# Degree power ahead of the border masks, constants and first tiles loaded as the first instructions, no clearing blocks

## The chip, the cores and the metric

One core of a Trainium2 chip. The metric is the device time of one execution in microseconds, the median of three runs. TensorE (PE) does the matmuls, VectorE (DVE), ScalarE (ACT) and GpSimd (POOL) the elementwise work, and SyncE (SP) issues the transfers. Each engine works through its own queue of instructions in order and waits on semaphores.

## What is computed

Four graph layers over x of 64 x 128 x 128 (batches, nodes, features) with one adjacency of 128 x 128. Each is followed by a residual sum and a layer norm. The first needs all eigenvectors U of a normalized Laplacian:

```python
deg = jnp.sum(A, axis=0) + jnp.sum(A, axis=1) - jnp.diagonal(A)
d_inv_sqrt = jnp.where(deg > 0, jax.lax.rsqrt(deg), 0.0)
L_norm = d_inv_sqrt[:, None] * (jnp.diag(deg) - A) * d_inv_sqrt[None, :]
_, U = jnp.linalg.eigh(L_norm)
h = jax.nn.relu(jnp.einsum('mn,bnd->bmd', U.T, x) @ W1 + b1)
x = _layernorm(x + jnp.einsum('nm,bmd->bnd', U, h @ W2 + b2))
x = _layernorm(x + gcn_then_lstm_over_windows(x, adj))   # windows of 1, 2, 3 and 4 nodes
x = _layernorm(x + graph_attention(x, adj))
x = _layernorm(x + four_head_masked_attention(x, adj))
```

## The kernel before

The program is a sequence of blocks. A block gives each engine a stream of instructions and ends in a barrier of all engines; the next block begins behind it.

**Block one**, `spectral_basis` (L52), makes the Laplacian and brings it to tridiagonal form in 127 reflections that are written out one after the other, with VectorE, TensorE, ScalarE and GpSimd working on each in turn. SyncE's part is one transfer, `A` (L129). GpSimd first fills tiles (L134 to L141), makes the identity and the triangle `below` (L143, L145), then six masks `blocks` (L151) and seven `borders` (L156, L159), and then raises the degrees to the power -0.5 (L162); after that come its two instructions of each reflection, `open_tail` (L167) and `open_gain` (L170). VectorE's path is: diagonal, row sums and degrees (L238 to L245), a wait for the power, and L248 to L258, which make the Laplacian M and the first reflection's column. `borders` is read in block two only.

**A clearing block** (`clear_semaphores`, L1434) follows block one, and another follows block two. GpSimd clears each semaphore that the block before it used, with one instruction each (L1438); the other engines go to the barrier at once.

**Block two**, `spectral_vectors` (L334). GpSimd makes tables (L408 to L424), on which VectorE waits (`tables`), and then seven `joins` (L427). TensorE and ScalarE build the basis in seven levels (L440 to L448), turn the constants of the layers (`turn`, after waiting for all 16 loads) and, once VectorE has finished its first count, multiply the features by W1 in 16 groups (`multiply`); the products go to DRAM and are read back later as `xw`. VectorE meanwhile finds the eigenvalues by counting sign changes (four counts) and makes the eigenvectors; the last instructions copy U and UT (L631, L632). SyncE's part: the 16 loads of the constants (`load`, L715), two `x_here` (L795), and then, for each group, the product's store and the load of the group after next (`transfer`, L798, L801).

**The layers** (`layers`, L836) run four trips over four slots of four batches each. The first trip's first stage is a matmul of `xw` with U in each slot (`hidden`; the helper's line is L1049). SyncE starts by loading `xin` (from x) and `xw` (the products) for the four slots (L1003, L1004); TensorE waits for both tiles of a slot and for a semaphore, `banks_free`, that VectorE raises as its first act:

```python
pe.wait_ge(x_in[s], trip * 32 + 32)
on("banks_free", s, trip)
each(P[s][1], lambda b: xw[s][:, b, :], lambda b: U[:]).then_inc(S_("hidden_ready"), 1)
```

Of the kernel before, what the change touches and what calls it, by code (L numbers as in the profile page):

```python
# [11 lines left out]
ALU = mybir.AluOpType  # L12
# [3 lines left out]
N = 128  # L16
# [34 lines left out]

def spectral_basis(nc, sb, psum, sem, adj_dram, A, ident_tail, ones, reflectors, gains, borders):  # L52

# [6 lines left out]
    E = sb("E", [N, N])  # L60
# [36 lines left out]
    stored = sem("stored")  # L97
    v_ready = sem("v_ready")
    row_copied = sem("row_copied")
# [14 lines left out]
    def col(j, n=1):  # L114
        return small[:, j:j + n]
# [10 lines left out]
    with nc.Block() as block:  # L126
        @block.sync
        def _(sp):
            sp.dma_start(A[:], adj_dram).then_inc(adj_in, 16)  # L129

        @block.gpsimd
        def _(pool):
            t = Tally(pool, pool_step)
            t.done(nc.gpsimd.memset(ident, 0.0))  # L134
            t.done(nc.gpsimd.memset(below[:], 1.0))
            t.done(nc.gpsimd.memset(ones[:], 1.0))
            t.done(nc.gpsimd.memset(tiny[:], 1e-30))
# [195 lines left out]

def spectral_vectors(nc, sb, psum, sem, ident, ones, E, D, reflectors, gains, borders, U, UT, constants, products):  # L334

# [51 lines left out]
    norm_ready = sem("ynorm_ready")  # L387
    y_ready = sem("y_ready")
    yT_ready = sem("yT_ready")
# [6 lines left out]

    load, turn, keep, mark = constants
# [239 lines left out]
G = 4  # L637
# [39 lines left out]

def load_constants(nc, c, sb_here, psum, sem, d, A, ident, ones):

# [6 lines left out]
    WT = sb_here("WT", [H, H])  # L686
    blockP = [psum(f"blockP{j}", [N, 512]) for j in range(4)]
    loads = sem("constants_in")
# [21 lines left out]
              (raw_b[:, 0, :], d["L1_gnn_bih"].rearrange("p (g r) -> (p g) r", r=H)),  # L710
              (raw_b[:, 1, :], d["L1_gnn_bhh"].rearrange("p (g r) -> (p g) r", r=H))]

    def load(sp):
# [58 lines left out]

    return load, turn, keep, mark


def feature_products(nc, sb, psum, sem, c, ident, x_dram, products_dram):

# [5 lines left out]
    made = [sb(f"made_{j}", [N, G, H]) for j in range(2)]  # L783
    acrossP = psum("acrossP", [N, 512])
    madeP = psum("madeP", [N, 512])
    fetched = [sem(f"fetched_{j}") for j in range(2)]
# [17 lines left out]

    def multiply(pe):
        for k in range(groups):
            j = k % 2
# [12 lines left out]

    def keep(act):
        for k in range(groups):
            j = k % 2
# [8 lines left out]

    return transfer, multiply, keep


def layers(nc, sb, psum, sem, c, ident, U, UT, x_dram, products_dram, out_dram):  # L836

    p4 = products_dram.rearrange("(t s g) n d -> t s n g d", s=SLOTS, g=G)
    x4 = x_dram.rearrange("(t s g) n d -> t s n g d", s=SLOTS, g=G)
    out4 = out_dram.rearrange("(t s g) n d -> t s n g d", s=SLOTS, g=G)  # L840
    GH = G * H
# [3 lines left out]

    xin = tiles("xin", [N, G, H])
    xw = tiles("xw", [N, G, H])
    x = tiles("x", [N, G, H])
# [35 lines left out]
    constant_ready = sem("constant_ready")  # L884
    x_in = [sem(f"x_in_{s}") for s in range(SLOTS)]
    y_out = [sem(f"y_out_{s}") for s in range(SLOTS)]
# [528 lines left out]
def program(nc, d, out):  # L1415
    from contextlib import ExitStack
    with ExitStack() as whole:
# [6 lines left out]
        def sem_of(stack):  # L1424
            def get(name):
                used.append(stack.enter_context(nc.semaphore(name)))
                return used[-1]
            return get

        used = []  # L1430
# [10 lines left out]
        sb = sb_of(whole)  # L1441
        A = sb("A", [N, N])
# [5 lines left out]
        c = hold_constants(sb)  # L1448
        products_dram = nc.dram_tensor("feature_products", (B, N, H), F32, kind="Internal").ap()
        with ExitStack() as spectrum:  # L1450
# [3 lines left out]
            borders = [held(f"borders_{1 << level}", [N, N]) for level in range(LEVELS)]  # L1454
            with ExitStack() as part:
                E, D = spectral_basis(nc, held, psum_of(part), sem_of(part), d["adj"], A, ident_tail, ones, reflectors, gains,
                                      borders)
                clear_semaphores()
            with ExitStack() as part:
                constants = load_constants(nc, c, sb_of(part), psum_of(part), sem_of(part), d, A, ident, ones)  # L1460
                products = feature_products(nc, sb_of(part), psum_of(part), sem_of(part), c, ident, d["x"], products_dram)
                spectral_vectors(nc, sb_of(part), psum_of(part), sem_of(part), ident, ones, E, D, reflectors, gains, borders,
                                 U, UT, constants, products)
                clear_semaphores()
        with ExitStack() as part:
            layers(nc, sb_of(part), psum_of(part), sem_of(part), c, ident, U, UT, d["x"], products_dram, out)

# [16 lines left out]
```

## Time and profile before

| | |
|---|---|
| three timed runs | 1472.52, 1474.07 and 1478.42 us, median 1474.07 |
| the profiled execution | span 1472.2 us, from its first to its last instruction; no other time of it is given |
| busy: PE, DVE, ACT, POOL | 1049.8, 1125.0, 803.6, 173.0 us |
| granted TensorE clock, mean | 0.895 |
| DMA packets | 25.51 MB, mean 17 GB/s |

The engines' busy times are sums over stages in which different engines lead, and they overlap. The chain of waits, which the profile follows back from the last instruction, reaches back to 670.2 us, the opening of the layers; what comes before it is read from the timeline and the waits.

### The profile page before, as it was taken

To read this page: it belongs to the slowest core of one execution; us is meant where nothing else is said; L and a number is where in the kernel's file an instruction comes from. 1 tells how busy PE (TensorE), PEld (TensorE's weight loads), DVE (VectorE), ACT (ScalarE), POOL (GpSimd) and SP (SyncE) were. 2 spreads that over 40 slices of the span, in tenths; PEclk is the share of its full clock that TensorE was granted. 3 is DMA by queue.
4 is the path that set the end of the run, shared out by engine and by line. 5 is a ranking of instruction groups with operands and counts; after the bars stand their busy time and mean duration, and the time that the engine had idled before them with its cause. 6 is when DMAs were issued, how large, how long until landed. Compare 5 with 4: busy or idle time off the path is not lost.

```text
span 1472.2 us, 24898 instructions
## 1 busy us (share of the span) xinstructions
PE 1049.8 (71%) x6161; PEld 862.0 (59%) x6161; DVE 1125.0 (76%) x5634; ACT 803.6 (55%) x2921; POOL 173.0 (12%) x464
## 2 busy tenths in 40 slices
PE   5777777777655600006998779988789978899875
PEld 4666666666544500005797566976668966679754
DVE  6888888888799889994457785576865578845687
ACT  3555555555322200003677866767767778677786
POOL 2111111111200000001011110111020120201111
PEclk9999999999986555557999999999899989999998
DMA  0000000000123400004000011000030000100001
GB/s 2 1 1 1 1 1 1 1 1 1 37 54 101 115 1 1 0 1 115 1 1 1 2 32 57 1 2 1 1 88 1 2 1 1 30 1 1 1 1 29
DMA packets 45246, 25.51 MB, mean 17 GB/s; under 512 B 1921, under 2 KB 44066, under 8 KB 45090
## 3 DMA queue, kind: packets, MB, share of 16 engines
q1 hardware_dynamic: 45090, 23.81, 5.8%
q8 instruction: 51, 0.84, 0.2%
q14 instruction: 105, 0.86, 0.2%
HBM read 15.42 MB, written 8.39 MB: 16 GB/s over the span
## 4 chain that ended last, share of the span: by engine, by line
PE 31%; DVE 11%; ACT 8%; issue 3%; POOL 1%; DMA 0%; DVEq 0%; POOLq 0%; ACTq 0%; SPq 0%
PE P L1101 11%; PE P L1109 6%; PE P L1049 6%; PE P L1054 2%; ACT x L1203 2%; ACT S L1271 2%; DVE stats L1310 2%; DVE S L1382 1%; DVE top L1387 1%; PE P L1163 1%; DVE t L1400 1%; PE P L1118 1%; PE P L1147 1%; POOL t L1037 1%; ACT t L1251 1%
## 5 line engine op out<-in xcount | busy, mean ns | idle before, releaser
L193 PE MATMUL productP<-M,ident_tail 128*128 128x127 f32 (+63 forms) x254 | 87.3, 441 | 71.2 <-DVE M L313 71.2
L1101 PE MATMUL P<-t,WihT 128*128 128x128 f32 (+1 forms) x832 | 119.4, 290 | 10.9 <-POOL t L1037 10.9
L1109 PE MATMUL P<-step_h,WhhT 128*128 128x128 f32 (+2 forms) x768 | 123.4, 304 | 0.0
L193 PEld LDWEIGHTS productP<-M,ident_tail 128*128 128x128 f32 x254 | 63.6, 311 | 95.0 <-DVE M L313 95.0
L1101 PEld LDWEIGHTS P<-t,WihT 128*128 128x128 f32 x832 | 109.9, 191 | 14.5 <-POOL t L1037 13.7
L1223 ACT ACTIVATE gate_i<-P,half_bias 128x128 f32<-128x128 f32 (+3 forms) x160 | 69.2, 433 | 88.9 <-PE P L1109 65.0
L1030 POOL TENSOR_TENSOR rstd<-variance,minus_half 128x4 f32<-128x4 f32 x64 | 64.5, 1008 | 430.8 <-DVE variance L1320 430.8
L1109 PEld LDWEIGHTS P<-step_h,WhhT 128*128 128x128 f32 x768 | 108.9, 191 | 4.5 <-DVE step_h L1353 0.7
L464 PE MATMUL sumP<-ident_tail,Yb 128*128 128x128 f32 x1 | 0.5, 473 | 153.2 <-DVE Yb L627 153.2
L190 PE MATMUL tailP<-ident_tail 128*128 128x128 f32 (+63 forms) x254 | 87.7, 443 | 19.9 <-DVE ident_tail L297 8.8
L1340 DVE SCALAR_TENSOR_TENSOR gate_i<-gate_i,gate_g 128x128 f32<-128x128 f32 (+2 forms) x96 | 36.1, 376 | 83.7 <-ACT gate_g L1223 83.7
L1271 ACT ACTIVATE S<-S,ntop 128x128 f32<-128x128 f32 x256 | 98.6, 390 | 0.0
L464 PEld LDWEIGHTS sumP<-ident_tail,Yb 128*128 128x128 f32 x1 | 0.2, 183 | 153.5 <-DVE Yb L627 153.5
L190 PEld LDWEIGHTS tailP<-ident_tail 128*128 128x128 f32 x254 | 63.6, 311 | 44.0 <-DVE ident_tail L297 42.9
L198 PE MATMUL p_rowP<-M,v_col 128*128 128x127 f32 (+63 forms) x254 | 84.9, 432 | 0.9 <-DVE v_col L282 0.7
L1101 PE MATMUL P<-HT,WihT 128*128 128x256 f32 (+1 forms) x288 | 84.7, 433 | 0.0
L220 ACT ACTIVATE small<-M,small 128x1 f32<-128x1 f32 x127 | 37.4, 294 | 84.2 <-DVE small L278 84.2
L494 ACT ACTIVATE small<-small 128x1 f32<-128x1 f32 x1 | 0.2, 203 | 149.1 <-DVE small L600 149.1
L1203 ACT ACTIVATE x<-x,shift,rstd 128x128 f32<-128x128 f32 x192 | 78.7, 483 | 4.3 <-POOL shift L1032 3.9
L215 ACT ACTIVATE row_square<-tailP 128x128 f32<-128x128 f32 (+63 forms) x127 | 28.8, 227 | 90.7 <-PE tailP L190 90.7
L1223 ACT ACTIVATE gate_o<-P,half_bias 128x128 f32<-128x128 f32 (+3 forms) x160 | 70.4, 440 | 8.5 <-PE P L1118 8.5
L1337 DVE SCALAR_TENSOR_TENSOR cell<-gate_i,gate_g 128x512 f32<-128x512 f32 (+3 forms) x64 | 27.9, 436 | 57.0 <-ACT gate_g L1223 56.4
(326 smaller groups left out, 3222.5 us busy)
## 6 DMA issues: line engine op xcount, KB each, us to landing
x_here<-x SPq DMA_DIRECT2D x16, 256.0 KB, 3.1
feature_products<-made SPq DMA_DIRECT2D x16, 256.0 KB, 2.4
xin<-x SPq DMA_DIRECT2D x16, 256.0 KB, 2.9
xw<-feature_products SPq DMA_DIRECT2D x16, 256.0 KB, 3.2
out<-y SPq DMA_DIRECT2D x16, 256.0 KB, 2.3
W<-L_gnn_W SPq DMA_DIRECT2D x3, 64.0 KB
Wqkv<-L_gnn_W SPq DMA_DIRECT2D x1, 192.0 KB
Wg<-L_gnn_Wg SPq DMA_DIRECT2D x2, 64.0 KB
```

Source lines behind the costliest of these rows:

```text
L190: pe.matmul(tailP[:, now:N + 1], tails, ident_tail[:, now:N + 1], start=True, stop=True).then_inc(tail_row_ready, 1)
L193: pe.matmul(productP[:, remaining], tails, M[:, remaining], start=True, stop=True).then_inc(product_ready, 1)
L198: pe.matmul(p_rowP[:, remaining], reflector, M[:, remaining], start=True, stop=True).then_inc(p_row_ready, 1)
L220: nc.scalar.activation(col(BETA_M), M[:, now:now + 1], ACT.Copy, scale=col(BETA)).then_inc(beta_m_ready, 1)
L1030: nc.gpsimd.tensor_tensor(rstd[s][:], variance[s][:], minus_half[:], ALU.pow).then_inc(S_("rstd_ready"), 1)
L1049: last = pe.matmul(out[:, b * H:(b + 1) * H], lhs(b), rhs(b), start=True, stop=True)
L1101: last = pe.matmul(place, c["WihT"][:, p - 1, gate * H:(gate + 1) * H], sources(s, p, t), start=bank not in fresh, stop=not t, skip_group_ ...
L1109: last = pe.matmul(gate_place(s, p, t, gate), c["WhhT"][:, p - 1, gate * H:(gate + 1) * H], step_h[s][:, 0:G * windows(p)], start=False, s ...
L1203: last = A_.activation(to[s][:, b, :], x[s][:, b, :], ACT.Identity, bias=shift[s][:, b:b + 1], scale=rstd[s][:, b:b + 1])
L1223: return A_.activation(tile[s][:, 0:m], gate_place(s, p, t, gate), ACT.Tanh, bias=bias[:, k:k + 1], scale=scale)
L1271: last = A_.activation(S[s][:, h, b, :], S[s][:, h, b, :], ACT.Exp, bias=ntop[s][:, k:k + 1], accum_out=total[s][:, k:k + 1])
L1340: V.scalar_tensor_tensor(gi[s][:, 0:m], gi[s][:, 0:m], 1.0, gg[s][:, 0:m], ALU.add, ALU.mult)
```

## The change

Three things. GpSimd computes the degree power right after the triangle masks, ahead of `blocks` and `borders`. SyncE issues the 16 constants, the first two `x_here` and the four first `xin` in block one, behind A, and the four first `xw` at the end of its part of block two; the layers' own first loads are gone. The clearing blocks are gone: all semaphores are taken for the whole program, and two that shared a name with one of the layers are renamed. The tiles that are loaded early are taken early too; the PSUM banks of the constants and the products are still taken in block two.

```diff
         def _(sp):
             sp.dma_start(A[:], adj_dram).then_inc(adj_in, 16)
+            for begin in fetch:
+                begin(sp)
...
             nc.gpsimd.memset(col(EXPONENT), -0.5).then_inc(masks_ready, 1)
+            pool.wait_ge(deg_base, 1)
+            nc.gpsimd.tensor_tensor(col(DI), col(DEG), col(EXPONENT), ALU.pow).then_inc(deg_root, 1)
             for level in range(1, LEVELS):
...
                 nc.gpsimd.tensor_tensor(borders[level][:], wider, blocks[level - 1][:], ALU.subtract)
-
-            pool.wait_ge(deg_base, 1)
-            nc.gpsimd.tensor_tensor(col(DI), col(DEG), col(EXPONENT), ALU.pow).then_inc(deg_root, 1)
...
         def _(sp):
-            load(sp)
             transfer(sp)
+            first_inputs(sp)
...
-    def transfer(sp):
+    def fetch(sp):
         for k in range(2):
             sp.dma_start(x_here[k][:], x_groups[k]).then_inc(fetched[k], 16)
+
+    def transfer(sp):
         for k in range(groups):
...
             on = waiter(sp)[0]
-            for s in range(SLOTS):
-                sp.dma_start(xin[s][:], x4[0, s]).then_inc(x_in[s], 16)
-                sp.dma_start(xw[s][:], p4[0, s]).then_inc(x_in[s], 16)
             with sp.Fori(0, TRIPS - 1) as i:
...
-        def clear_semaphores():
-
-            with nc.Block() as block:
-                @block.gpsimd
-                def _(pool):
-                    for semaphore in used:
-                        pool.sem_clear(semaphore)
-            used.clear()
...
+        def first_residuals(sp):
+            for s in range(SLOTS):
+                sp.dma_start(xin[s][:], by_slots(d["x"])[0, s]).then_inc(x_in[s], 16)
+
+        def first_products(sp):
+            for s in range(SLOTS):
+                sp.dma_start(xw[s][:], by_slots(products_dram)[0, s]).then_inc(x_in[s], 16)
+
...
                 E, D = spectral_basis(nc, held, psum_of(part), sem, d["adj"], A, ident_tail, ones, reflectors, gains,
                                       borders, (load, fetch, first_residuals))
-                clear_semaphores()
...
                 spectral_vectors(nc, sb_of(part), psum_of(part), sem, ident, ones, E, D, reflectors, gains, borders,
                                  U, UT, constants, products, first_products)
-                clear_semaphores()
```

## Rows read from the trace of the kernel before

**Rows 1.** Busy time in stretches: TensorE, its loads, VectorE, ScalarE, GpSimd; clock; DMA.

```profile
393.00:667.00 274.00, 74.90 (x306) 58.23 (x306) 256.34 (x1619) 32.56 (x76) 7.06 (x20) 0.59 0.16 42
667.00:670.20 3.20, 0.00 (x0) 0.00 (x0) 0.06 (x1) 0.00 (x0) 0.00 (x0) 0.50 0.00 0
674.00:680.00 6.00, 5.22 (x24) 4.93 (x25) 0.69 (x1) 0.69 (x1) 0.00 (x0) 0.52 0.86 225
680.00:1472.00 792.00, 683.17 (x4811) 561.29 (x4809) 537.60 (x1711) 573.35 (x1826) 109.80 (x160) 0.95 0.05 15
```

**Rows 2.** Timeline of the start: start, duration, engine, line [idle before <-releaser].

```profile
2.58 2.39 POOL L151 TENSOR_SCALAR_AFFINE_SELECT blocks<-below 128x128 f32<-128x128 f32 x6
...
2.73 0.65 DVE L238 TENSOR_SCALAR spark<-ident_tail 128x128 f32<-128x128 f32 x1 [2.73 <-POOL small L148]
...
3.82 0.15 DVE L244 TENSOR_SCALAR small<-small 128x1 f32<-128x1 f32 x1
...
7.37 0.46 POOL L159 TENSOR_TENSOR borders<-below,blocks 128x128 f32<-128x128 f32 x1
7.78 0.56 POOL L162 TENSOR_TENSOR small<-small 128x1 f32<-128x1 f32 x1
8.45 0.16 DVE L248 TENSOR_TENSOR small<-small 128x1 f32<-128x1 f32 x1 [4.41 <-POOL small L162]
8.64 0.29 DVE L249 TENSOR_SCALAR scrap<-ident_tail,small 128x128 f32<-128x128 f32 x1
...
11.39 0.22 DVE L258 SCALAR_TENSOR_TENSOR ident_tail<-M,below,spark 128x1 f32<-128x1 f32 x1
...
13.81 0.19 POOL L170 TENSOR_TENSOR open_gain<-inverses,below 128x1 f32<-128x1 f32 x1 [1.93 <-DVE inverses L280]
```

**Rows 3.** Timeline of the seam between block one and block two.

```profile
389.32 0.29 DVE L324 COPY D<-tailP 128x128 f32<-128x128 f32 x1 [0.89 <-PE tailP L202]
...
393.08 0.50 PEld L433 LDWEIGHTS sumP<-reflectors 128*128 128x128 f32 x2 [4.10 <-issue]
393.10 0.45 POOL L408 TENSOR_TENSOR T<-ident_tail,gains 128x128 f32<-128x128 f32 x1 [6.94 <-POOLq L1434]
```

**Rows 4.** Waits of SyncE's queue: us in total, times, longest.

```profile
SPq L126 <- PEq L126: 388.7, 1, 388.7
...
SPq L400 <- PEq L400: 152.8, 1, 152.8
...
SPq L1434 <- PEq L1434: 5.8, 2, 2.9
```

**Rows 5.** The clearing instructions: count, ns min/median/max, first and last start.

```profile
L1438 POOLq EVENT_SEMAPHORE_RANGE_CLEAR  x72: 44/44/48, 390.1 to 669.9; - x72
```

**Rows 6.** Timeline of the seam between block two and the layers.

```profile
666.78 0.28 DVE L632 COPY UT<-outP 128x128 f32<-128x128 f32 x1
670.26 0.38 SPq L1003 DMA_DIRECT2D xin<-x  x1
...
670.70 0.50 SPq L1004 DMA_DIRECT2D xw<-feature_products  x1
...
673.44 0.51 SPq L1003 DMA_DIRECT2D xin<-x  x1
...
673.95 2.08 PE L1049 MATMUL P<-U,xw 128*128 128x128 f32 x8 [7.42 <-DMA xw<-feature_products]
```

**Rows 7.** Timeline of SyncE's issues in block two, the first and the x_here.

```profile
393.07 0.82 SPq L715 DMA_DIRECT2D W<-L_gnn_W  x2
...
407.40 0.97 SPq L795 DMA_DIRECT2D x_here<-x  x2
```

**Rows 8.** DMA issues: tile, count, size, us from issue to landing.

```profile
A<-adj SPq DMA_DIRECT2D x1, 64.0 KB, 1.8
```

**Rows 9.** Timeline of TensorE in block two, the first matmul of four levels.

```profile
398.21 0.77 PE L440 MATMUL sumP<-T,joins 128*128 128x128 f32 x2 [0.46 <-ACT TT L476]
...
401.43 0.77 PE L440 MATMUL sumP<-T,joins 128*128 128x128 f32 x2 [0.46 <-ACT TT L476]
...
411.11 0.77 PE L440 MATMUL sumP<-T,joins 128*128 128x128 f32 x2 [0.46 <-ACT TT L476]
...
414.34 0.77 PE L440 MATMUL sumP<-T,joins 128*128 128x128 f32 x2 [0.46 <-ACT TT L476]
```

**Rows 10.** The chain of waits at the layers' first back edge.

```profile
877.46 2.75 issue
```

More of the change, by code:

```diff
@@ L49, in step, with spectral_basis @@
         self.wait()
-def spectral_basis(nc, sb, psum, sem, adj_dram, A, ident_tail, ones, reflectors, gains, borders):
+def spectral_basis(nc, sb, psum, sem, adj_dram, A, ident_tail, ones, reflectors, gains, borders, fetch):
     ident = ident_tail[:, 0:N]
@@ L97, in spectral_basis @@
     stored = sem("stored")
-    v_ready = sem("v_ready")
+    v_ready = sem("reflector_ready")
     row_copied = sem("row_copied")
@@ L331, in reversed_columns, with spectral_vectors @@
     return bass.AP(ap.tensor, ap.offset + (n - 1) * step, [[p_step, p], [-step, n]])
-def spectral_vectors(nc, sb, psum, sem, ident, ones, E, D, reflectors, gains, borders, U, UT, constants, products):
+def spectral_vectors(nc, sb, psum, sem, ident, ones, E, D, reflectors, gains, borders, U, UT, constants, products,
+                     first_inputs):
     QT = sb("QT", [N, N])
@@ L387, in spectral_vectors @@
     norm_ready = sem("ynorm_ready")
-    y_ready = sem("y_ready")
+    y_ready = sem("vectors_signed")
     yT_ready = sem("yT_ready")
@@ L395, in col @@
         return small[:, j:j + 1]
-    load, turn, keep, mark = constants
+    turn, keep, mark = constants
     transfer, multiply, keep_products = products
@@ L675, in hold_constants, with load_constants @@
     return c
-def load_constants(nc, c, sb_here, psum, sem, d, A, ident, ones):
+def load_constants(nc, c, sb_here, sem, d, A, ident, ones):
     a12 = c["a12"]
@@ L686, in load_constants @@
     WT = sb_here("WT", [H, H])
-    blockP = [psum(f"blockP{j}", [N, 512]) for j in range(4)]
+    blockP = []
     loads = sem("constants_in")
@@ L711, in load_constants, with banks @@
               (raw_b[:, 1, :], d["L1_gnn_bhh"].rearrange("p (g r) -> (p g) r", r=H))]
+    def banks(psum):
+        blockP.extend(psum(f"blockP{j}", [N, 512]) for j in range(4))
     def load(sp):
@@ L771, in mark, with feature_products @@
         nc.gpsimd.tensor_scalar(c["mask"][:], A[:], 0.0, MASKED, ALU.is_equal, ALU.mult)
-    return load, turn, keep, mark
-def feature_products(nc, sb, psum, sem, c, ident, x_dram, products_dram):
+    return banks, load, turn, keep, mark
+def feature_products(nc, sb, sem, c, ident, x_dram, products_dram):
     groups = B // G
@@ L783, in feature_products @@
     made = [sb(f"made_{j}", [N, G, H]) for j in range(2)]
-    acrossP = psum("acrossP", [N, 512])
-    madeP = psum("madeP", [N, 512])
+    held_banks = []
     fetched = [sem(f"fetched_{j}") for j in range(2)]
@@ L791, in feature_products, with banks @@
     made_kept = sem("made_kept")
-    def transfer(sp):
+    def banks(psum):
+        held_banks.extend(psum(name, [N, 512]) for name in ("acrossP", "madeP"))
+    def fetch(sp):
         for k in range(2):
             sp.dma_start(x_here[k][:], x_groups[k]).then_inc(fetched[k], 16)
+    def transfer(sp):
         for k in range(groups):
@@ L805, in multiply @@
     def multiply(pe):
+        acrossP, madeP = held_banks
         for k in range(groups):
@@ L821, in keep @@
     def keep(act):
+        acrossP, madeP = held_banks
         for k in range(groups):
@@ L831, in keep, with input_tiles, by_slots, layers @@
             nc.scalar.activation(made[j][:].rearrange("n g h -> n (g h)"), madeP[:], ACT.Copy).then_inc(made_kept, 1)
[L833 to L840, printed above, removed]
+    return banks, fetch, transfer, multiply, keep
+def input_tiles(sb, sem):
+    xin, xw = ([sb(f"{name}_{s}", [N, G, H]) for s in range(SLOTS)] for name in ("xin", "xw"))
+    return xin, xw, [sem(f"x_in_{s}") for s in range(SLOTS)]
+def by_slots(dram):
+    return dram.rearrange("(t s g) n d -> t s n g d", s=SLOTS, g=G)
+def layers(nc, sb, psum, sem, c, ident, U, UT, x_dram, products_dram, out_dram, inputs):
+    p4, x4, out4 = (by_slots(dram) for dram in (products_dram, x_dram, out_dram))
+    xin, xw, x_in = inputs
     GH = G * H
@@ L844, in tiles @@
         return [sb(f"{name}_{s}", shape) for s in range(SLOTS)]
-    xin = tiles("xin", [N, G, H])
-    xw = tiles("xw", [N, G, H])
     x = tiles("x", [N, G, H])
@@ L884, in layers @@
     constant_ready = sem("constant_ready")
-    x_in = [sem(f"x_in_{s}") for s in range(SLOTS)]
     y_out = [sem(f"y_out_{s}") for s in range(SLOTS)]
@@ L1424, in sem_of @@
         def sem_of(stack):
[L1425 to L1430, printed above, removed]
-        def clear_semaphores():
-            with nc.Block() as block:
-                @block.gpsimd
-                def _(pool):
-                    for semaphore in used:
-                        pool.sem_clear(semaphore)
-            used.clear()
-        sb = sb_of(whole)
+            return lambda name: stack.enter_context(nc.semaphore(name))
+        sb, sem = sb_of(whole), sem_of(whole)
         A = sb("A", [N, N])
@@ L1449, in program @@
         products_dram = nc.dram_tensor("feature_products", (B, N, H), F32, kind="Internal").ap()
+        inputs = input_tiles(sb, sem)
+        xin, xw, x_in = inputs
+        def first_residuals(sp):
[4 more added lines that the diff above has]
+                sp.dma_start(xw[s][:], by_slots(products_dram)[0, s]).then_inc(x_in[s], 16)
         with ExitStack() as spectrum:
@@ L1454, in program @@
             borders = [held(f"borders_{1 << level}", [N, N]) for level in range(LEVELS)]
+            constant_banks, load, *constants = load_constants(nc, c, held, sem, d, A, ident, ones)
+            product_banks, fetch, *products = feature_products(nc, held, sem, c, ident, d["x"], products_dram)
             with ExitStack() as part:
-                E, D = spectral_basis(nc, held, psum_of(part), sem_of(part), d["adj"], A, ident_tail, ones, reflectors, gains,
-                                      borders)
-                clear_semaphores()
+                E, D = spectral_basis(nc, held, psum_of(part), sem, d["adj"], A, ident_tail, ones, reflectors, gains,
+                                      borders, (load, fetch, first_residuals))
             with ExitStack() as part:
[L1460 to L1463, printed above, removed]
-                clear_semaphores()
+                constant_banks(psum_of(part))
+                product_banks(psum_of(part))
+                spectral_vectors(nc, sb_of(part), psum_of(part), sem, ident, ones, E, D, reflectors, gains, borders,
+                                 U, UT, constants, products, first_products)
         with ExitStack() as part:
-            layers(nc, sb_of(part), psum_of(part), sem_of(part), c, ident, U, UT, d["x"], products_dram, out)
+            layers(nc, sb_of(part), psum_of(part), sem, c, ident, U, UT, d["x"], products_dram, out, inputs)
 NAMES = ("x", "adj", "L0_gnn_W1", "L0_gnn_b1", "L0_gnn_W2", "L0_gnn_b2", "L1_gnn_Wg0", "L1_gnn_bg0", "L1_gnn_Wg1",
```

## The prediction

> **What bounds the kernel now.** I read the stretches first. The span falls into three blocks of the program, one after the other, and no engine works in the seams between them: from 667.0 to 670.2 us all five together are busy for 0.06 us [rows 1]. In the reflections (up to 389.6) and in block two (393 to 667) a serial chain on VectorE sets the pace, with TensorE, ScalarE and GpSimd answering; in the layers (from 670) TensorE leads. The change touches none of the long loops. It works on four short places where everything stands still, so I read the timeline of each.
>
> The first is the start. VectorE has the degrees ready at 3.97 (L244, 3.82 + 0.15) and next runs L248 at 8.45; its wait, 4.41 us, is ended by GpSimd's power L162. That instruction needs only the degrees, but stands in GpSimd's queue behind the masks L151 to L159, which end at 7.83 [rows 2]. Nothing else can run: the Laplacian and the first reflection follow from L248.
>
> The second and third are the seams. D is copied by 389.61 and the next block's first instructions start at 393.07 to 393.10 [rows 3, 7]; UT is copied by 667.06 and the layers' first instruction starts at 670.26 [rows 6]. SyncE's waits say what lies between: 5.8 us in two waits, at most 2.9 each, on L1434, the clearing block [rows 4]; in it GpSimd issues 72 clears one by one [rows 5]. Of the seams' 3.46 and 3.20 us, 0.56 and 0.30 are left for the end of the block itself.
>
> The fourth is the first matmul of the layers: SyncE issues xin at 670.26 and xw at 670.70, and TensorE starts at 673.95, released by xw [rows 6].
>
> **The degree power.** Only its place changes: one instruction of 0.56 us. From L162's end (8.34) to L248 (8.45) the hand-over takes 0.11. In the new place the power starts at about 3.97 + 0.1, ends at 4.63, and L248 starts at 4.74: 3.71 us earlier. Against this, six affine selects, a copy and six subtractions, 5.2 us of GpSimd (2.58 to 7.83), now run beside VectorE's Laplacian instead of before it. What that costs is shown by one pair: L238, a 128x128 tensor-scalar, took 0.65 us beside an affine select, and L249, the same operation and shape with GpSimd at nothing but the finished power, 0.29 [rows 2]: 0.36 us for one meeting. Of the path's full-width instructions there are four (L249, L253, L255, L256) and one narrow one with SBUF inputs alone (L258); L251 runs beside a matmul. So the collisions cost between 0 and 5 x 0.36 = 1.8 us. Conversely L238 loses its own collision, since GpSimd then waits for the degrees: up to 0.36 back, if TensorE's column sum isn't later. I take 0.5 for the net loss, nearer to the small end because the narrow L244 took 0.15 beside the same selects: gain 3.2, bounds 1.9 and 4.1.
>
> The Trainium skill (SBUF — State Buffer, "Who interferes with whom") speaks against this move: VectorE and GpSimd share a port pair under an exclusive lock, and the later instruction waits for the whole of the other; it exempts VectorE instructions with one SBUF input outside the two-port modes. The trace agrees that a meeting costs about one instruction's length: 0.36 us, where six selects took 2.39 [rows 2]. By that rule L253 and L255, each with one PSUM input, go free, three meetings stay at 0.36, and the gain is 2.6, the sum 11.9.
>
> Behind the masks, GpSimd's first two instructions of the reflections wait in the same queue. The masks end near 4.63 + 5.2 = 9.8. The first open_gain (L170), now at 13.81, is due at about 10.6 [rows 2]. So 0.8 us of slack covers them; collisions longer than that delay one reflection once.
>
> **The clearing blocks.** Both go with their barriers. The 72 clears and their hand-over are SyncE's 5.8 us of waiting [rows 4, 5], and no other engine works meanwhile [rows 1, 3]. What stays is the block's own end, the 0.56 and 0.30 above. Gain 5.8. The upper bound is 6.1, if part of those 0.86 us belongs to the second barrier. The lower bound comes from instructions that aren't at hand on entering a block: the only such row is the loop's back edge in the layers, where the chain shows 2.75 us of "issue" [rows 10]. Twice that leaves 0.3.
>
> **The first tiles.** All eight loads leave the layers' head: xin is loaded in block one, xw at the end of SyncE's part of block two. The first matmul then needs only U, copied before the block ends, and a bank semaphore that VectorE raises on entry. From the opening (670.26) it came 3.69 us late; TensorE's own first instruction in block two came within 0.05 us of SyncE's [rows 3, 7]. I leave 0.2 for the semaphore: gain 3.5, bounds 3.0 and 3.7. The other slots' tiles are needed later still, and are then long there. Six more loads follow the first pair and no later pass waited for them, so they give nothing more.
>
> **What moves at no price.** SyncE's queue gets 22 more issues behind A in block one: 16 constants, two x_here, four xin. In block two the constants and x_here take from 393.07 to 408.37, 15.3 us [rows 7]; with four more of about 0.5 each SyncE ends near 18.5, while it now waits 388.7 us for the end of the block [rows 4]. In block two the constants were not waited for either, and the products begin after the first count on VectorE, so their earlier loads gain nothing. At the end of block two four xw issues follow the last stored product; SyncE has 152.8 us of waiting there [rows 4]. Without this cover the 18 us would be paid in full. The new traffic meets the first reflections. A chain of TensorE, ScalarE and GpSimd results ran beside the same loads in block two: one level of joins took 3.22 us during them (398.21 to 401.43) and 3.23 after them (411.11 to 414.34) [rows 9]. So I take 0.
>
> **The clock.** At the start of the layers TensorE runs at 1.2 GHz (granted clock 0.50 to 0.52 until 680, 0.95 on average after) [rows 1]. Its first eight matmuls took 2.08 us [rows 6]; at 2.4 GHz, half, 1.04. Three such passes fall before 680, so 3.1 us hang on when the clock rises. It now stands idle for a shorter time before them, and where the rise falls against the start is not shown: 0 taken, bounds minus 3.1 and plus 3.1.
>
> **Sum.** 3.2 + 5.8 + 3.5 = 12.5 us. The profiled execution's span of 1472.2 becomes 1459.7. The page gives no other time of that execution; the fastest timed run (1472.52) is 0.3 above the span, the median (1474.07) 1.9. Against the median the sum gives 1461.6 us.
>
> **The rivals.**
> *Cold entries.* The clears hide the fetching of the next block's instructions. For it: the 2.75 us at the back edge [rows 10]. Against it: at the ends of the blocks, before the clears, only 0.56 and 0.30 us pass, and three engines entered block two within 0.04 us [rows 3, 6, 7]. The Trainium skill (Runtime: NRT & Kernel Launch, "Instruction fetch mechanics") says that fetching runs ahead in sequence and only a taken branch to a distant page stalls; no run here shows yet which of the two a block's end is. At 2 x 2.75 the gain is 12.5 - 5.5 = 7.0: 1467.1.
> *Collisions eat the power's gain.* The masks beside the Laplacian and the first reflection cost as much as the wait did, 3.2: 1464.8. For it the 0.65 against 0.29; against it that the path has only five such instructions.
> *The first matmul waits for something else.* If another releaser comes just as late as xw, 3.5 is lost: 1465.1. Nothing in the rows names one.
> *A arrives late.* On the other side. 22 loads stand right behind A on the same queue. If A finished only with them, everything would begin later: the issues alone take 17.3 us, and A now lands 1.8 us after its issue [rows 8], so some 17 us late: 1474.1 - 12.5 + 17 = 1478.6, slower. It decides from 12.5 us of delay on. Against it: in the layers the first xin and xw released TensorE 3.25 us after xw's issue, with five more loads queued behind them already [rows 6]; later loads don't hold up an earlier one by anything near that.
>
> **Chances.** Forecast 0.74; cold entries 0.08; collisions 0.08; another wait 0.05; A late 0.05. A measurement here can tell about 0.5%, 7.4 us. The forecast, the collisions and the other wait lie beyond it, 0.87, of which I give 0.02 to scatter: faster 0.85. Cold entries and part of a late A stay within it: same 0.12. Slower 0.03. The range: at the top the cold entries, 1467.1; at the bottom the upper bounds 4.1 + 6.1 + 3.7 = 13.9 and half the clock's 3.1, 1458.6, and 1.9 less if the median falls as near the span as the fastest run did: 1456.7. I say 1456.5 to 1467.5.
>
> **What would show it.** L248 starts at 4.7 to 5.0 and the first reflection's L258 near 8.4 instead of 11.39; L249 to L258 take longer than now by 0 to 0.36 each. No L1434 in SyncE's waits; the seams shrink to about 0.6 and 0.4. The first L1049 starts within 0.3 us of the layers' opening, and its idle time is ended by VectorE, not by xw. From there on the layers should last as long as before, give or take the clock. The prediction is wrong if A lands after 3 us, if a seam holds over 1 us of "issue", or if the layers' trips change by more than about 3 us in all.

## The result and the profile after

The changed kernel takes 1462.4 us, the median of four runs (1460.09 to 1462.97), against 1473.61 us for the kernel before (four runs, 1472.52 to 1478.42). The ratio is 0.9907 with a 95% interval of 0.9887 to 0.9928: some 1% faster, by 10.6 to 16.7 us (the two medians lie 11.2 us apart). The forecast was 1461.6.

The profiled execution of the changed kernel has a span of 1458.2 us and is the run of 1460.09, so 1.9 us of its time lie outside the span. The profile of before has 1472.2: the difference to explain is 14.0 us. I cut both spans at five events that every trace has (VectorE's copies of D and UT, the first `p_row` matmul, T's start, the first matmul of U and xw); the table also holds the experiments of the next section.

| profile | start, to the first p_row | reflections, to D copied | seam 1, to T | block two, to UT copied | seam 2 and tiles, to the first U, xw | layers | span |
|---|---|---|---|---|---|---|---|
| before | 13.81 | 375.80 | 3.49 | 273.96 | 6.89 | 798.21 | 1472.2 |
| after | 10.59 | 375.53 | 0.54 | 272.88 | 0.49 | 798.15 | 1458.2 |
| e1 power only | 10.45 | 375.53 | 3.49 | 272.74 | 7.42 | 799.95 | 1469.6 |
| e2 no clears only | 13.80 | 375.56 | 0.53 | 272.95 | 3.91 | 800.68 | 1467.4 |
| e3 first tiles only | 13.78 | 375.55 | 3.49 | 272.76 | 3.40 | 804.64 | 1473.6 |
| e4 constants back | 10.56 | 375.57 | 0.54 | 272.75 | 0.49 | 801.07 | 1461.0 |
| e5 masks spread | 9.93 | 375.80 | 0.54 | 272.91 | 0.49 | 804.96 | 1464.6 |
| e6 bare blocks | 10.62 | 375.84 | 0.87 | 273.28 | 0.79 | 800.29 | 1461.7 |
| e7 rounds written out | 10.64 | 375.83 | 0.54 | 262.92 | 0.45 | 802.30 | 1452.7 |
| e8 adjacency last | 32.86 | 375.82 | 0.54 | 273.50 | 0.46 | 798.09 | 1481.3 |

Of the 14.0 us, 3.22 come from the start, 2.95 from seam 1, and 6.40 from seam 2 with the tiles: 12.57 in the places that the change works on. The rest is 0.27 in the reflections, 1.08 in block two and 0.06 in the layers.

The timeline of the start after (start, duration, engine, line; lines have moved by one and more, so L248 of before is L249):

```profile
0.81 0.39 SPq L129 DMA_DIRECT2D A<-adj  x1
...
1.26 0.89 SPq L720 DMA_DIRECT2D W<-L_gnn_W  x2
...
2.84 0.23 DVE L239 TENSOR_SCALAR spark<-ident_tail 128x128 f32<-128x128 f32 x1 [2.84 <-DMA A<-adj]
...
3.81 0.15 DVE L245 TENSOR_SCALAR small<-small 128x1 f32<-128x1 f32 x1
...
4.05 0.56 POOL L152 TENSOR_TENSOR small<-small 128x1 f32<-128x1 f32 x1 [1.42 <-DVE small L245]
...
4.58 2.39 POOL L155 TENSOR_SCALAR_AFFINE_SELECT blocks<-below 128x128 f32<-128x128 f32 x6
4.72 0.32 DVE L249 TENSOR_TENSOR small<-small 128x1 f32<-128x1 f32 x1 [0.69 <-POOL small L152]
...
5.08 0.30 DVE L250 TENSOR_SCALAR scrap<-ident_tail,small 128x128 f32<-128x128 f32 x1
5.28 0.50 DVE L252 SCALAR_TENSOR_TENSOR scrap<-ident_tail,small,A 128x128 f32<-128x128 f32 x1
...
6.34 0.35 DVE L254 SCALAR_TENSOR_TENSOR scrap<-scrap,small,tailP 128x128 f32<-128x128 f32 x1 [0.56 <-PE tailP L182]
...
7.25 0.29 DVE L256 TENSOR_TENSOR scrap<-scrap,productP 128x128 f32<-128x128 f32 x1 [0.57 <-PE productP L184]
...
7.86 0.31 DVE L259 SCALAR_TENSOR_TENSOR ident_tail<-M,below,spark 128x1 f32<-128x1 f32 x1
...
9.35 0.45 POOL L163 TENSOR_TENSOR borders<-below,blocks 128x128 f32<-128x128 f32 x1
9.43 0.38 DVE L274 SCALAR_TENSOR_TENSOR small<-row_square 128x1 f32<-128x1 f32 x1 [1.26 <-ACT row_square L216]
...
10.59 0.79 PE L199 MATMUL p_rowP<-M,v_col 128*128 128x127 f32 x2 [0.93 <-DVE v_col L283]
```

VectorE's wait for the power has shrunk from 4.41 us to 0.69, and L249 starts 3.73 us earlier than in [rows 2]. A lands at 2.84, and at 2.83 in e2 of the next section, which has no loads behind it: they did not hold it up. L239's own collision is gone (0.23 us instead of 0.65), but that gave nothing back here: it starts at 2.84 instead of 2.73, and the degrees are ready at 3.96, as before. (In e1 it starts at 2.67, and the power 0.15 us earlier than here.) The masks run from 4.58 to 9.80 beside the Laplacian, and four of VectorE's instructions are longer for it: L249 (0.32), L252 (0.50), L259 (0.31) and, a step into the first reflection, L274 (0.38). What they cost is settled by e5 below.

The timelines of the two seams after, the first and then the second:

```profile
385.83 0.29 DVE L325 COPY D<-tailP 128x128 f32<-128x128 f32 x1 [0.89 <-PE tailP L203]
386.65 0.50 PEld L435 LDWEIGHTS sumP<-reflectors 128*128 128x128 f32 x2 [1.15 <-issue]
386.66 0.45 POOL L410 TENSOR_TENSOR T<-ident_tail,gains 128x128 f32<-128x128 f32 x1 [3.98 <-POOLq L126]
...
659.26 0.28 DVE L634 COPY UT<-outP 128x128 f32<-128x128 f32 x1
659.81 0.10 POOL L1038 MEMSET minus_half<- 128x4 f32 x1 [266.03 <-POOLq L402]
660.00 1.78 PEld L1064 LDWEIGHTS P<-U,xw 128*128 128x128 f32 x8 [1.28 <-issue]
660.03 2.05 PE L1064 MATMUL P<-U,xw 128*128 128x128 f32 x8 [1.01 <-DVEq L1304]
```

GpSimd's first instruction of the next block follows the last copy by 0.54 and 0.27 us, against 3.49 and 3.21 before (T at 393.10 in [rows 3], and 670.27, just behind SyncE's first issue in [rows 6]), and the layers' first matmul comes 0.22 us behind the opening, released by VectorE's queue (the bank semaphore) and no longer by xw. SyncE's waits after have the same two long ones as [rows 4], and none at a clearing block:

```profile
SPq L126 <- PEq L126: 365.8, 1, 365.8
...
SPq L402 <- PEq L402: 151.2, 1, 151.2
```

The wait at the end of block one is 22.9 us shorter: 3.5 us because the block ends earlier (386.12 instead of 389.61), the rest because SyncE issues the 22 loads in that time. Nobody waits for them.

The layers open at the same low clock as in [rows 1]: the stretches of seam 2, of the first 6 us of the layers and of the rest, after (clock is the number behind GpSimd's busy time):

```profile
659.20:659.90 0.70, 0.00 (x0) 0.00 (x0) 0.34 (x2) 0.00 (x0) 0.09 (x1) 0.50 0.00 0
660.00:666.00 6.00, 5.19 (x24) 4.93 (x25) 0.69 (x1) 0.69 (x1) 0.00 (x0) 0.53 0.01 3
666.00:1458.00 792.00, 686.05 (x4811) 562.99 (x4809) 537.35 (x1711) 573.36 (x1826) 109.62 (x160) 0.95 0.05 15
```

One thing in block two I had not read before predicting. These are VectorE's longest waits for nothing that the profile shows ("issue"): total, times, longest, first before and then after.

```profile
DVE shift L551 <- issue: 7.3, 2, 4.2
```

```profile
DVE shift L553 <- issue: 6.3, 2, 3.2
DVE stats L1325 <- issue: 4.9, 2, 2.5
DVE inverse L517 <- issue: 2.4, 12, 0.2
```

The counting of eigenvalues and the layers are loops on VectorE. Each taken back edge holds it up for about 3 us, and in the profile of before one of them took 1.0 us more: that is block two's 1.08. The change did not shorten it: e9, the changed kernel again, has one of 4.1 us, and its block two takes 273.83.

### The profile page after: what moved, and what is told of

It reads as the page before. It is cut to its first block, busy times and chain, and to the rows that moved or that the text cites. A ratio compares the mean times of both kernels' runs of the same rounds, so it can differ in the third digit from the quotient of the medians.

```text
span 1458.2 us, 24803 instructions
## 1 busy us (share of the span) xinstructions
PE 1051.9 (72%) x6161; PEld 863.0 (59%) x6161; DVE 1125.1 (77%) x5634; ACT 803.5 (55%) x2921; POOL 172.3 (12%) x464
## 4 chain that ended last, share of the span: by engine, by line
PE 31%; DVE 11%; ACT 8%; issue 3%; POOL 1%; DVEq 0%; POOLq 0%; ACTq 0%
PE P L1116 11%; PE P L1124 6%; PE P L1064 6%; PE P L1069 2%; ACT x L1218 2%; ACT S L1286 2%; DVE stats L1325 2%; DVE S L1397 1%; PE P L1178 1%; DVE top L1402 1%; DVE t L1415 1%; PE P L1133 1%; PE P L1162 1%; POOL t L1052 1%; ACT t L1266 1%
```

## The experiments

**Each part alone.** e1 is the kernel before with the power moved:

```diff
             nc.gpsimd.memset(col(EXPONENT), -0.5).then_inc(masks_ready, 1)
+            pool.wait_ge(deg_base, 1)
+            nc.gpsimd.tensor_tensor(col(DI), col(DEG), col(EXPONENT), ALU.pow).then_inc(deg_root, 1)
...
-            pool.wait_ge(deg_base, 1)
-            nc.gpsimd.tensor_tensor(col(DI), col(DEG), col(EXPONENT), ALU.pow).then_inc(deg_root, 1)
```

> The kernel before with the degree power alone moved ahead of the masks. Theory (the four parts add up, each in its own place): L248 starts near 4.6 us instead of 8.45, collisions give back 0.5, so the first p_row matmul (L198) starts near 10.5 instead of 13.81, and the span is 3.3 us shorter (3.0 to 3.7); the seams stay at 3.46 and 3.20 us and the first xw wait at 3.69. The adjacency has no loads behind it here, so VectorE's L238 starts at 2.73 as before, not at 2.84. Rival (the masks cost elsewhere what the power gains): span within 0.5 us of before.

e2 is the kernel before without the clearing blocks (two semaphores renamed, all taken for the whole program):

```diff
-                clear_semaphores()
...
-                clear_semaphores()
```

> The kernel before without the two clearing blocks, nothing else. Theory: 2.95 us at each seam, 5.9 us in all; the seams shrink to about 0.5 and 0.3 us from the last copy to the next block's first instruction. The tiles' wait at the layers' head stays 3.7 us. Rival (entries into a block are slow once the clears don't cover them, at the 2.75 us of a back edge): at most 0.4 us in all.

e3 is the kernel before with the layers' first eight loads at the end of SyncE's part of block two:

```diff
             transfer(sp)
+            first_inputs(sp)
...
-            for s in range(SLOTS):
-                sp.dma_start(xin[s][:], x4[0, s]).then_inc(x_in[s], 16)
-                sp.dma_start(xw[s][:], p4[0, s]).then_inc(x_in[s], 16)
```

> The kernel before with xin and xw of the first trip loaded at the end of SyncE's part of block two; constants, power and clears as before. Theory: the first matmul of the layers starts 0.2 to 0.3 us after their opening instead of 3.69, 3.45 us gained, and nothing more. Rival (another releaser is as late as xw): the first matmul still starts over 3 us after the opening, 0 gained.

Measured against the kernel before, ten runs each: e1 0.9978 (0.9960 to 0.9997), e2 0.9962 (0.9945 to 0.9980), e3 0.9973 (0.9955 to 0.9991). Of 1477.19 us that is 3.2, 5.6 and 4.0 us; the three together 12.8, and the change itself gave 13.7 (0.0093 of 1473.61). Each of the three is known to some 2.7 us only, so the sum proves little; the traces are finer. The table places each: e1 gains 3.36 us at the start and nothing in the seams (its xw even landed 0.53 later); e2 gains 2.96 in seam 1 and 2.98 in seam 2, and its tiles are still late; e3 gains 3.49 between the end of block two and the first matmul. Together that is 12.79, against 12.57 with all three in one kernel: the parts add up, and none stands in another's way.

**The moved loads.** e4 is the changed kernel with the constants and `x_here` loaded in block two again; the first `xin` stay in block one.

```diff
         def _(sp):
+            for begin in early:
+                begin(sp)
             transfer(sp)
...
-                                      borders, (load, fetch, first_residuals))
+                                      borders, (first_residuals,))
...
-                                 U, UT, constants, products, first_products)
+                                 U, UT, constants, products, first_products, (load, fetch))
```

> The changed kernel with the 16 constants and the two x_here loaded at the head of block two again; only xin stays in block one. Theory (moving these loads gives nothing, they were covered in both places): the same time as the changed kernel, 0 to 0.2 us less at the start because fewer loads stand behind the adjacency. Rival 1 (the loads in block two slowed VectorE there): 1 us or more slower than the changed kernel, in block two. Rival 2 (the shorter first back edge of VectorE's loop in the changed kernel, 3.01 against 3.99 us, comes from the earlier loads): that edge goes back to 4 us.

1462.1 us, ratio 0.9910 (0.9874 to 0.9946). Start, reflections, seams and block two are within 0.13 us of those after. The 18 issues give nothing and cost nothing in either place, and both rivals fall: block two takes 272.75 us, and its longest back edge 3.1 (3.2 after).

**The collisions.** e5 is the changed kernel with the mask work taken out of the start: one select, copy or subtraction behind `open_gain` of each of the reflections 1 to 13, counted from 0.

```diff
+            def mask(k):
+                if 1 <= k < LEVELS:
...
+                elif k == LEVELS:
...
+                elif LEVELS < k < 2 * LEVELS:
...
                 nc.gpsimd.tensor_tensor(open_gain[:], inverses[:, 1:2], below[:, now:now + 1],
                                         ALU.mult).then_inc(open_gain_ready, 1)
+                mask(k)
```

> The changed kernel with the thirteen mask instructions taken out of the start and issued one by one after open_gain of the reflections 1 to 13, where GpSimd waits anyway. Theory (the masks beside the Laplacian cost VectorE 0.5 us by collisions): L249 back from 0.32 to 0.16 us, the first narrow instruction of the first reflection from 0.38 to 0.16; the first p_row matmul starts 5.3 to 5.4 us after the power's VectorE successor instead of 5.87, as in the kernel before (5.36); 0.5 us gained there, and 0 to 0.5 lost again in the thirteen reflections. Rival (the 5.87 has another cause, such as the loads that now arrive in these microseconds): it stays at 5.8 to 5.9.

The timeline of its start: the four instructions that were longer after, one that reads PSUM (L258), and the matmul that ends the stretch:

```profile
4.57 0.16 DVE L253 TENSOR_TENSOR small<-small 128x1 f32<-128x1 f32 x1 [0.69 <-POOL small L152]
...
4.97 0.35 DVE L256 SCALAR_TENSOR_TENSOR scrap<-ident_tail,small,A 128x128 f32<-128x128 f32 x1
...
6.01 0.35 DVE L258 SCALAR_TENSOR_TENSOR scrap<-scrap,small,tailP 128x128 f32<-128x128 f32 x1 [0.70 <-PE tailP L186]
...
7.51 0.22 DVE L263 SCALAR_TENSOR_TENSOR ident_tail<-M,below,spark 128x1 f32<-128x1 f32 x1
...
8.99 0.16 DVE L278 SCALAR_TENSOR_TENSOR small<-row_square 128x1 f32<-128x1 f32 x1 [1.26 <-ACT row_square L220]
...
9.93 0.80 PE L203 MATMUL p_rowP<-M,v_col 128*128 128x127 f32 x2 [0.71 <-DVE v_col L287]
```

From the power's first user to the first `p_row` matmul it takes 5.36 us (4.57 to 9.93), as before (8.45 to 13.81); after the change it is 5.87 (4.72 to 10.59). So the masks beside the Laplacian cost 0.51 us. The loads are no part of it: e1, which has none behind A, takes 5.89 (4.56 to 10.45). Spread over the reflections the masks cost nothing: 375.80, where e6, e7 and e8 of the same chip take 375.82 to 375.84. Its one run, 1466.53 us, shows none of this, because its layers are 6.8 us longer than those after; of that below.

**The bare block.** e6 is the changed kernel with a block at each seam in which GpSimd clears one spare semaphore, and nothing else is done.

```diff
+        def bare_block():
+            with nc.Block() as block:
+                @block.gpsimd
+                def _(pool):
+                    pool.sem_clear(spare)
...
+                bare_block()
...
+                bare_block()
```

> The changed kernel with a block of a single clear put back at each of the two seams. Theory (the clears, issued one by one, are most of the 2.95 us): each seam grows by 0.4 to 0.6 us, to about 1.0 and 0.75, so about 2.4 to 2.5 us of each old seam were the other 34 and 36 clears, 0.07 us each. Rival (a block costs its barrier, whatever is in it): each seam grows by over 2 us.

```profile
386.17 0.29 DVE L325 COPY D<-tailP 128x128 f32<-128x128 f32 x1 [0.89 <-PE tailP L203]
...
387.33 0.46 POOL L410 TENSOR_TENSOR T<-ident_tail,gains 128x128 f32<-128x128 f32 x1 [4.32 <-POOLq L1446]
...
660.33 0.28 DVE L634 COPY UT<-outP 128x128 f32<-128x128 f32 x1
...
661.40 0.98 PE L1064 MATMUL P<-U,xw 128*128 128x128 f32 x3 [1.32 <-DVEq L1304]
```

Seam 1 is 0.87 us instead of 0.54; from UT's copy to the first matmul it is 0.79 instead of 0.49. One more block with its barrier costs 0.33 and 0.30 us, less than the 0.4 to 0.6 expected. The rest of each removed clearing block, some 2.6 us, was the clears themselves, issued one by one: of the 2.95 and 2.94 us saved, 89% and 90%.

**The adjacency last.** e8 is the changed kernel with A's transfer behind the 22 loads, which makes the rival's case real.

```diff
-            sp.dma_start(A[:], adj_dram).then_inc(adj_in, 16)
             for begin in fetch:
                 begin(sp)
+            sp.dma_start(A[:], adj_dram).then_inc(adj_in, 16)
```

> The changed kernel with the adjacency issued behind the other 22 loads instead of ahead of them. This prices the rival of a late A. Theory (SyncE issues one after the other, and everything at the start waits for A): A is issued near 18 us, VectorE's first instruction starts near 20.5 instead of 2.84, and the span grows by 17 to 18.5 us, to about 1476. Rival (SyncE's issues run ahead of the transfers, so that A costs its own 1.8 us wherever it stands): under 3 us more.

The timeline of e8's start, SyncE's queue and VectorE's first instruction:

```profile
7.76 4.75 SPq L720 DMA_DIRECT2D raw_h<-L_gnn_Whh  x1
12.56 3.38 SPq L720 DMA_DIRECT2D raw_b<-L_gnn_bih  x1
...
17.46 3.00 SPq L1456 DMA_DIRECT2D xin<-x  x4
20.50 0.80 SPq L131 DMA_DIRECT2D A<-adj  x1
25.11 0.23 DVE L239 TENSOR_SCALAR spark<-ident_tail 128x128 f32<-128x128 f32 x1 [25.11 <-DMA A<-adj]
```

VectorE starts 22.3 us later than after (25.11 against 2.84), more than the 17 to 18.5 expected, and 1483.26 us was the one run's time, 20.9 above the changed kernel's median. A is issued at 20.50, 19.7 us later, and needs 4.6 us instead of 2.0 from there. Of these 2.6 us more, 0.4 are a longer issue (0.80 instead of 0.39); that the rest is A's transfer waiting behind those in front is likely, but not shown. That A comes first in the queue is therefore worth more than the whole change.

**The back edges.** e7 is the changed kernel with the rounds of the eigenvalue counting written out on VectorE, the same arithmetic.

```diff
-            with v.Fori(0, ROUNDS) as r:
+            for r in range(ROUNDS):
```

> The changed kernel with the three refinement rounds of VectorE in block two written out instead of looped. Theory (a taken back edge of that long loop stalls VectorE for its next instructions, 2.8 to 3.1 us in six profiles, and VectorE sets the end of block two): two edges go, block two takes 267 us instead of 272.8, and the kernel is 5.7 us faster than the changed one. Rival (the stall is the fetching of so much code and comes back wherever the code is new): block two within 1 us of 272.8.

1455.48 us, ratio 0.9855 (0.9834 to 0.9877). Block two takes 262.92 us instead of 272.88, 9.96 less, where 5.7 were expected: the edges alone had been counted. VectorE's groups in the same stretch of block two, 430 to 640 us: after, and then e7 (count | busy, mean ns | idle before, and what ended it).

```profile
L517 DVE RECIPROCAL inverse<-q 128x16 f32<-128x16 f32 x189 | 46.6, 247 | 2.5 <-issue 2.4
...
L553 DVE TENSOR_SCALAR shift<-frac,small 128x16 f32<-128x16 f32 x3 | 0.9, 294 | 6.5 <-issue 6.3 <-DVE small L546 0.2
```

```profile
L517 DVE RECIPROCAL inverse<-q 128x16 f32<-128x16 f32 x189 | 46.7, 247 | 0.1
...
L553 DVE TENSOR_SCALAR shift<-frac,small 128x16 f32<-128x16 f32 x3 | 0.9, 294 | 0.1
```

Busy times are equal; the idle is gone. The two edges are 6.3 us and twelve bubbles at L517 are 2.4, together 8.7 of the 9.96. Over all of block two VectorE's idle time falls by 8.8 us; the other 1.2 are busy time (256.5 and 255.3 us), too thinly spread to show in a group. The timed runs gained less: the median lies 6.9 us below the changed kernel's 1462.4. In e7's profile the layers take 802.30 us, against 798.15 after.

**The changed kernel again, and further.** e9 is the changed kernel unaltered, on the chip of e10 and e11. e10 joins e5 and e7. e11 also writes out the layers' trips on all engines:

```diff
-        with engine.Fori(0, TRIPS - 1) as i:
-            following = engine.snap(i + 1)
+        for i in range(TRIPS - 1):
+            following = i + 1
```

> The changed kernel again, on the chip and against the runs of this call. Theory (12.5 to 13 us from four places, with the layers between 798 and 805 us whatever the change did): ratio 0.990 to 0.993.

> The changed kernel with the masks spread over the reflections and the three rounds of VectorE written out. Theory (both act where VectorE sets the pace, and add): 0.6 + 9.9 = 10.5 us less than the changed kernel; in the profile the first p_row matmul at 9.9 to 10.1 us, block two 262.9 us. Rival (a part is given back in the other's place): less than 9 us.

> The same with the four trips of the layers written out as well, so that no engine has a loop. Theory (VectorE's two back edges of 2.9 us in the layers, the 'issue' of the chain of waits, go; TensorE's, ScalarE's and GpSimd's edges of 0.3 us are hidden): layers 4 to 6 us shorter than in the kernel above, beyond their own spread of 798 to 805. Rival (TensorE leads in the layers and fills VectorE's pause with work that is at hand): under 2 us.

Against 1477.82 us for the kernel before: e9 1462.45, ratio 0.9905 (0.9888 to 0.9922); e10 1454.95, 0.9848 (0.9834 to 0.9861); e11 1446.74, 0.9783 (0.9764 to 0.9801). e9 repeats the result. In e10 the first `p_row` starts at 9.98 and block two takes 262.95: both gains stand together. The medians of e9 and e10 lie 7.5 us apart, and the ratios 8.4, where 10.5 were expected and the rival (a part is given back) stood under 9. In the two profiles 0.6 and 10.9 us are gained at these places, and the layers are 4.6 us longer in e10 (803.21 against 798.64). Whether they gave something back or scattered isn't settled. In e11 VectorE has no "issue" wait left at the layers' norms, and the layers take 795.36 us, the shortest of all these profiles. Its median lies 8.2 us below e10's; the two back edges that it takes out were 5.1 us of VectorE's waits in e10, and 2.0 of TensorE's and 1.5 of ScalarE's, which go too. But the gain doesn't lie where the edges stood, near the start of the second and the third trip: by trips it is 0.7, 0.2, 3.7 and 3.2 us, and in the last two the granted clock is higher (0.97 and 0.95 against 0.95 and 0.92). So what the layers' edges are worth stays open, for the reason that comes next.

**What the layers add by themselves.** With equal work they take 798.1 to 805.0 us in the table. From each trip's first matmul of U and xw to the next, the two middle trips take 197.5 to 198.5 us in every profile of the table and in e9 and e10, while the last one, to the end, takes either 207.2 to 207.4 or 210.6 to 210.9, and the first 194.4 to 198.0. The last trip after, and then in e10 (TensorE's busy time first, the clock behind GpSimd's):

```profile
1250.94:1458.18 207.24, 172.95 (x1214) 141.82 (x1212) 141.35 (x459) 147.37 (x468) 31.18 (x46) 0.93 0.04 11
```

```profile
1242.14:1452.95 210.81, 175.85 (x1214) 143.93 (x1212) 141.62 (x459) 147.15 (x468) 31.13 (x46) 0.92 0.04 11
```

The same 1214 matmuls keep TensorE busy 2.9 us longer, and the granted clock is a hundredth lower, so more of this stretch lies at the lower of its two levels (1.2 instead of 2.4 GHz): 28 us of it after, and 35 in e10. Why isn't settled: the layers' code is the same in these kernels, and the profiles of before, after, e1, e2, e4, e6, e8 and e9 fall on the short side, those of e3, e5, e7 and e10 on the long one. It is scatter of up to 3.7 us each in the first and the last trip that no part of the change explains.

## Why the prediction was right

**The sum.** 12.5 us were predicted for four places, and these measured 12.57 in the traces; e1, e2 and e3 gave 12.8, by their traces and by the timed ratios. The median came out 0.8 us above the forecast; so close a hit is partly luck, since the layers alone scatter by 7 us.

**The degree power: 3.2 predicted, 3.22 measured (3.36 in e1).** L249 starts at 4.72, where 4.74 was worked out, and the net loss to collisions is 0.51 against 0.5 taken. Their makeup was not the one I described. I expected full-width instructions to be hit; L250, one of them, took 0.30 beside the selects, against 0.29 without them in [rows 2]; it is the operation and shape of L238 (its scalar a column, L238's a constant), so the 0.65 against 0.29 from which a meeting was priced at 0.36 did not repeat. The two with a PSUM input, L254 and L256, kept 0.35 and 0.29. What grew, each against e5, were L252 by 0.15, which lies beside the matmul of tailP, and three narrow ones on the path: L249 by 0.16, L259 by 0.09 and L274, in the first reflection, by 0.22, together 0.47 of the 0.51. The size was right; that narrow instructions go nearly free, from which I took the small end, was not: L244, from which I read it, has one SBUF input. The Trainium skill (SBUF — State Buffer, "Who interferes with whom") says that an instruction of VectorE with two SBUF inputs contends with GpSimd's reads and one with a single SBUF input need not; the four that grew take two inputs from SBUF, and L254 and L256, which take one there and one from PSUM, kept their time, so the trace agrees. By the rule as the prediction used it, three meetings at 0.36, the loss would be 1.1; the delays were 0.09 to 0.22.

**The clearing blocks: 5.8 predicted, 5.89 measured.** Each seam keeps the block's own end, 0.54 and 0.27, where 0.56 and 0.30 were read. e6 splits the gain: 0.63 for the two blocks with their barriers, the rest for the clears.

**The first tiles: 3.5 predicted, 3.46 measured (3.49 in e3, where both tiles load at the end of block two).** The matmul comes 0.22 us behind the opening, where 0.2 was left for the bank semaphore, and its releaser is the one named.

**What moves at no price: shown.** In e4 it makes no difference where the constants load. The reflections, which now run beside the transfers, are 375.53 against 375.80.

**The clock: 0 taken.** The layers are 0.06 us shorter. The first passes run at the low level as before (0.53 against 0.52), and the idle time removed in front of them bought or cost nothing that can be told from the 7 us by which the layers scatter. Where the rise falls was left open, and the two traces tell it: the granted clock goes from 0.50 to 1.00 (1.2 to 2.4 GHz) some 5.9 us behind the layers' first matmul before (679.8) and 5.6 after (665.7). That these two agree is luck too, for in the table's other profiles it is 6.1 to 8.9. The sign of being wrong that was set at 3 us in the layers is smaller than their scatter.

**The rivals.** Cold entries are refuted: with no clears in front of it a block's first instruction follows within 0.54 us, in after and in e2. "Collisions eat the power's gain" has a sixth of its price: 0.51 of 3.2. "The first matmul waits for something else": no, by the profile's releaser. "A arrives late" did not occur (A lands 2.0 us after its issue), but e8 shows that its price was too small: 22.3 us, not 17, since the loads in front take 19.7 us to issue, not 17.3, and A then needs 2.6 us more. Of the issues, `raw_h` took 4.75 us there, against 3.48 before, and the four `xin` 3.00, where 0.5 each was taken.

**What it did not see.** The profile's 14.0 us hold 1.4 beyond the four places, mostly one back edge that was 1.0 us longer in the profile of before. Scatter of one execution lies in a difference of two profiles; the ratio's interval, 10.6 to 16.7 us, is the measure.

## What to carry to other kernels

Where every engine stands still, a gain added one to one here, and the timeline of that place priced it to some tenths of a microsecond: read the seams between blocks before the loops. Clearing semaphores one by one between two blocks costs as many instructions as there are semaphores, on a path that nothing covers; a block with its barrier costs a tenth of that. Loads may stand behind the transfer that opens the kernel, but not ahead of it (22.3 us in e8); and a loop whose body is written for few rounds is worth pricing against writing the rounds out.

## What the runs showed of the hardware

A taken back edge holds up the three engines whose loop body is long, not only VectorE. The trace has records of the branches, which the views leave out; from the branch to the first instruction of the next round it takes VectorE 2.8 to 4.0 us (bodies of 526 and 580 instructions), ScalarE 2.5 to 2.9 (533) and TensorE 3.4 to 4.1 (2483, with its weight loads) in all the profiles, register instructions counted; GpSimd (74) and SyncE (38) go on after 0.2 to 0.3. What TensorE and ScalarE start meanwhile stood in their queues ahead of the branch, and it covers most of the time; the 0.3 us of e11's expectation were the way to these, not to the next round. What is left uncovered shows in the waits after (total, times, longest), and is gone in e11:

```profile
PE P L1083 <- issue: 2.2, 2, 1.2
ACT L1223 <- issue: 1.4, 2, 0.7
```

The Trainium skill (Runtime: NRT & Kernel Launch, "Instruction fetch mechanics") says that a taken branch to code outside the window that is held stalls on fetching, and gives this as a reason to unroll fully. The trace agrees in that the long bodies stall and the short ones don't, and e7 in that the rounds written out don't; no run here separates fetching from another cost that grows with the body.

Inside the looped counting rounds there are twelve waits of 0.2 us for nothing that the profile shows, which go when the rounds are written out (idle before L517 2.5 us, then 0.1).

One instruction of SyncE that issues a load can take several us: `raw_h` 2.6 to 5.0 in these runs (4.75 in e8) and the first half of `raw_b` 3.3 to 3.4, where an `xin` took 0.75 (3.00 for four). Its own size doesn't tell: `raw_x`, of the shape of `raw_h`, took 0.84, and the second half of `raw_b`, as large as the first, 0.41. The two long ones stand, in every run, right behind the two largest loads, `raw_x` and `raw_h` (1 MB each by their shapes); why is not shown.
